# Three pieces of work in another order in a two-layer block on one core: a load ahead of two stores, a difference ahead of an eviction, half of a gram ahead of a mix

## The reference

```python
def layer0(v, gamma):                      # v = _gn(x)
    a = v.reshape(b, h * w, c)
    attn = softmax(einsum('bpi,bpj->bij', a, a))
    return gamma * einsum('bpc,bcj->bpj', a, attn) + a

def layer1(v, ...):                        # v = _gn(x + layer0)
    v = (v - v.min()) / (v.max() - v.min() + EPS)         # over each image
    measures = [box_sum(v, k) for k in (2, 4, 8, 16)]
    log_m = log(measures + EPS)
    alphas = einsum('bhwcs,s->bhwc', log_m, lr_c) / sum(lr_c ** 2)
    excite = sigmoid(relu(alphas.mean(h, w) @ w1 + b1) @ w2 + b2)
    sim = correlation of log_m with its fitted line
    return sim * sigmoid(bn(alphas)) + (1 - sim) * v * excite

x = x + layer0(_gn(x)); x = x + layer1(_gn(x))
```

## Time and profile before

| | |
|---|---|
| median of 3 timed runs | 6843.75 us (6843.52 to 6863.24) |
| the profiled execution | 6870.93 us, its span 6869.2 us |
| busy share of the span | VectorE 80%, TensorE 74%, ScalarE 70%, GpSimd 26% |
| DMA | 1344.69 MB moved, mean 196 GB/s |
| 695 us of turn 6 | VectorE busy 636.19, TensorE 581.42, ScalarE 579.68; granted clock 0.97 |

### The profile page before, as it was taken

How to read it: one execution, slowest core, us unless ns; L and a number is a source line. 1 busy time by engine, 2 the same in 40 slices (tenths; PEclk the granted TensorE clock), 3 DMA queues, 4 the chain that set the end, 5 groups by cost and what they waited for, 6 DMA issues and landing times. The chain is left out here.

```text
span 6869.2 us, 108733 instructions
## 1 busy us (share of the span) xinstructions
PE 5112.8 (74%) x35320; PEld 4647.5 (68%) x35320; DVE 5524.0 (80%) x6453; ACT 4827.6 (70%) x5203; POOL 1757.7 (26%) x1201
## 2 busy tenths in 40 slices
PE   6968886788858888588867888588885777466643
PEld 6757776677747777477766777477774666466642
DVE  1359998689969999699986999689996999699961
ACT  0118887588848888488875888488884888588861
POOL 0022221422232222322213222322223222333310
PEclk9989998899979999799988999799997999788875
DMA  3635554577746777477755777467774666456656
GB/s 117 195 114 166 176 171 130 176 232 240 230 148 214 226 232 230 132 235 230 223 190 169 238 241 228 148 208 228 236 230 126 219 221 220 159 170 187 189 176 230
DMA packets 874516, 1344.69 MB, mean 196 GB/s; under 512 B 38705, under 2 KB 694097, under 8 KB 857937
## 3 DMA queue, kind: packets, MB, share of 16 engines
q1 hardware_dynamic: 837456, 1208.16, 51.7%
q0 software_dynamic: 36864, 134.23, 10.3%
HBM read 671.16 MB, written 536.87 MB: 176 GB/s over the span
## 5 line engine op out<-in xcount | busy, mean ns | idle before, releaser
L530 PE MATMUL even<-band,t 128*128 128x128 f32 x12288 | 1867.0, 283 | 473.9 <-ACT logs L706 293.3
L530 PEld LDWEIGHTS even<-band,t 128*128 128x128 f32 x12288 | 1625.7, 197 | 548.6 <-issue 444.4
L387 POOL TENSOR_TENSOR t<-t 128x1024 f32<-128x1024 f32 (+3 forms) x800 | 1337.3, 1683 | 1451.3 <-DVE logs L979 1408.3
L511 PE MATMUL h_ps<-mix,xt 128*128 128x256 f32 x4096 | 1054.6, 403 | 454.0 <-DVE mx L891 327.3
L511 PEld LDWEIGHTS h_ps<-mix,xt 128*128 128x128 f32 x4096 | 773.8, 199 | 603.0 <-ACT xt L693 310.7
L428 POOL DMA_DIRECT2D x1t<-logs x256 | 226.4, 884 | 2882.9 <-DVE ut L990 2815.4
L706 ACT ACTIVATE logs<-even,col 128x1024 f32<-128x1024 f32 x512 | 568.8, 1111 | 444.6 <-PE even L530 443.2
L532 PE MATMUL even<-band,t 128*128 128x128 f32 x4096 | 792.0, 275 | 0.0
L891 DVE CUSTOM_DVE_ANT_0 h_out<-h_ps,shift,mx 128x512 f32<-128x512 f32 x512 | 382.7, 748 | 488.5 <-PE h_ps L511 487.5
L488 PE MATMUL g_ps<-xa 128*128 128x257 f32 x2048 | 634.8, 391 | 152.4 <-DMA xa<-in_x_dram 152.1
L532 PEld LDWEIGHTS even<-band,t 128*128 128x128 f32 x4096 | 621.9, 192 | 0.0
(11 more groups left out here) (184 smaller groups left out, 10492.4 us busy)
## 6 DMA issues: line engine op xcount, KB each, us to landing
xa<-in_x_dram SPq DMA_DIRECT2D x256, 512.0 KB, 4.5
xb<-in_x_dram SPq DMA_DIRECT2D x256, 512.0 KB, 5.5
h_scratch<-h_out SPq DMA_DIRECT2D x128, 1024.0 KB, 7.7
hr<-h_scratch SPq DMA_DIRECT2D x256, 512.0 KB, 6.0
q_scratch<-ut SPq DMA_DIRECT2D x256, 512.0 KB, 2.7
x1t<-logs POOLq DMA_DIRECT2D x256, 512.0 KB, 5.1
p_scratch<-x1t SPq DMA_DIRECT2D x256, 512.0 KB, 3.1
pd<-p_scratch SPq DMA_DIRECT2D x256, 512.0 KB, 6.1
```

The source lines that it names most:

```text
L387: ins = g.tensor_tensor(dst[:, hf, d:d + n, :], src[:, hf, d:d + n, :], src[:, hf, e:e + n, :], ALU.add)
L511: ins = t.matmul(h_ps[:, r * C:(r + 1) * C], xt[:, q % 2, jh, r, :], mix[:, jh, :], start=(jh == 0), stop=(jh == 1))
L530: ins = t.matmul(o, src[:, hf, at, :], band[:, which, :], start=True, stop=(which < 3))
```

## The change

Three edits, none of which adds or removes an instruction. On SyncE the load of h's rows, with its wait, goes ahead of the stores of h and out. On TensorE the second half of the gram goes from its place before box 3 to one between turn_back 0 and mix 2. On VectorE the third difference goes ahead of the second eviction of h_ps.

```diff
@@ SyncE, half_chunk
                     sp.dma_start(pd[:, hf, :], p_dram[ud]).then_inc(pq_loaded[hf], 16)
                     sp.dma_start(qd[:, hf, :], q_dram[ud]).then_inc(pq_loaded[hf], 16)
+                if Cs and not (began and hf == 0) and not (last and (k, hf) != (0, 0)):
+
+                    sp.wait_ge(odd_filled, 2 * u)
+                    apart()
+                    if hf == 1:
+                        load_rows(nC + 2, 1 - k, 0)
+                    else:
+                        load_rows(nC + 1, k, 1)
                 if Bs and hf == 0 and not began:
                     sp.wait_ge(h_copied, 4 * nb + 1)
                     apart()
...
                     sp.wait_ge(o_copied, 4 * nd + 1)
                     apart()
                     sp.dma_start(out_chunk[nd - 1], o_sb[:, 1 - k, :, :]).then_inc(o_stored[1 - k], 16)
-                if Cs and not (began and hf == 0) and not (last and (k, hf) != (0, 0)):
-
-                    sp.wait_ge(odd_filled, 2 * u)
-                    apart()
-                    if hf == 1:
-                        load_rows(nC + 2, 1 - k, 0)
-                    else:
-                        load_rows(nC + 1, k, 1)
                 if Cs and not began:
                     store_pq(u - 2, nC - 1, hf)
@@ TensorE, half_chunk
                     box(u, k, hf, 2)
                     box(u, k, hf, 1)
-                if A:
-                    gram_rows(n, hf, 1)
                 if Cs:
                     box(u, k, hf, 3)
...
                 if Ds:
                     turn_back(2 * nd + hf, hf, 0)
+                if A:
+                    gram_rows(n, hf, 1)
                 if Bs:
                     mix_x(nb, 2 * hf + 1)
@@ VectorE, half_chunk
                 if Cs:
                     low_contrasts(u, hf)
+                    high_contrast(u, hf)
                 if Bs:
                     copy_h(nb, k, 2 * hf + 1, first, None)
-                if Cs:
-                    high_contrast(u, hf)
                 if Bs:
                     min_h(i, k, hf)
```

## The result

The changed kernel takes 6643.64 us (four runs, 6641.73 to 6644.86), the one before 6843.64 us beside it (four runs, 6837.24 to 6863.24). The ratio is 0.9703, with a 95% interval of 0.9683 to 0.9723: 200 us faster. The forecast was 6637 us. Measured again beside the last experiments, against 6864.12 us for the kernel before, it took 6650.82 us, ratio 0.9697 (0.9678 to 0.9717).

What follows compares the result with a forecast made beforehand. VectorE was taken as the bound, so its waits could be won: 127 + 64 + 20 + 7 - 11 = 207 us off the timed median of 6843.75 us gives 6637 us, range 6598 to 6730 us, held at 78%.

Steps and rivals of the forecast that it cites:

- The bound: VectorE, busiest engine at 80% of the span, bounds the kernel with 21.1 us of work per half-chunk.
- The load of h's rows, 127 us: SyncE: issued ahead of both stores, the load lands in time and all L927 waits go, 127 us (low end 107).
- The reason of place: SyncE's queue: 2 MB of stores ahead made the load take 10.6 us against 5.9; moving it ahead gains 2.6 us.
- The waits for h_ps in full turns, 64 us: VectorE, turns 3 to 7: with the third difference first, copy_h's waits of 75 us shrink by 64 (low end 30).
- Turn 2, 20 us: VectorE, turn 2: of 41.8 us of waits for h_ps, mix 1's half stays; 20 us won, bounds 0 and 40.
- it starts only 0.15 us earlier, and TensorE idles there for the rest: TensorE: with the gram half moved away, box 3 still waits for log 2, so it gains only 0.15 us.
- The minimum behind the eviction, 11 us against: VectorE: min_h directly after the eviction it reads costs 0.05 us in 224 half-chunks, 11 us; bounds 0 and 25.
- Starts of turns, 7 us: TensorE, starts of turns 2 to 7: box 3 no longer behind the gram half; 7 us won, bounds 0 and 8.
- The load came earlier: Answers the rival that turn_h or the queue holds the load of h's rows: 127 us stay, 6764 us; 6%.
- the 6 us that I had named as a warning: Sign that the prediction is wrong: a summing DMA taking over 6 us.
- the 4.0 us of delay: Rival, stores stretch the summing DMA by 4.7 us, deciding from 4.0 us on: 62 us slower, 6906 us; 4%.
- The path behind xa: Rival: loop over summing DMA, SyncE, xa and mix 1, 20.5 us a half-chunk, takes over; 6757 us, 12%.

Runs made afterwards that it cites:

- the short minimum: Changed kernel with VectorE's minimum over h_out reading 16 elements per half-chunk instead of 1024 (values differ): 6484.07 us, ratio 0.9452 to the kernel before.
- The early xa: Changed kernel with the minimum cut to 16 elements and SyncE loading xa and xb ahead of the p and q stores: 6465.94 us, ratio 0.9427.

## Why the prediction was right, and where its terms were off

- **The bound.** VectorE at 21.1 us a half-chunk, with little beside it: turn 3 was to take 658 us and took 657.8. The clock of 1.00 over turn 3 is what I expected as well.
- **The load of h's rows, 127 us.** All waits went, and the part alone is worth 133 us. On top of the other two it is worth 110 to 115, since it and they share some 20 us. The load shown lands 7.8 us after issue where I allowed 8, 2.7 us early where I had 2.6. The reason of place was over-weighed: with one store ahead it would still have come in time. The earlier issue and the place of either store each did a part.
- **The waits for h_ps in full turns, 64 us.** They fell from 77.0 to 16.0 us, 61. With this term, the load's share in these turns (122 us) and 8 of the 11 us against, the five turns were to shorten by some 178 us; they did by 176.5. A wait of 2.2 us a turn was to stay, for mix 1 at the turn's start, and it did.
- **Turn 2, 20 us: this term was mis-sized.** I wrote "that half stays" of the waits for mix 1. They fell from 22.0 to 6.3 us, and the turn lost 35.1 us. The step that failed is that of the gram half leaving its old place: "it starts only 0.15 us earlier, and TensorE idles there for the rest", read from one half-chunk in which log 2 came late. The run without the gram's move shows the waits for mix 1 back (23.3 us). That half-chunk was not the rule even in its own turns: in each full turn of the trace before, box 3 started more than 0.5 us after log 2 had ended in 20 to 23 of 31 half-chunks.
- **The minimum behind the eviction, 11 us against: it came, a little larger.** The lists show no wait of L900, as they leave out idle times up to 0.15 us, but in the full turns it starts 0.12 us after the end of the instruction ahead of it, at the mean, where it had started 0.08 ahead of that end. The third difference wins 0.12 us of these 0.20 back in its new place. VectorE's time per half-chunk of the full turns, less its waits for h_ps and h's rows, is 21.13 us in the changed kernel and 21.06 without the difference's move: 0.07 us, some 15 in all.
- **Starts of turns, 7 us.** The stretches between the turns are 9 us shorter than before; without the gram's move all but 1 to 2 us of that is lost.
- **The rivals.** The load came earlier. The summing DMA takes 5.1 us at the median of the full turns and up to 6.6; 13 of 150 are over the 6 us that I had named as a warning, and before they were 12, up to 6.9. So the stores behind the load did not stretch it, and the 4.0 us of delay never came. The path behind xa is real, but in the changed kernel it cost at most some 2 us a full turn.

In sum the terms came to 207 us, measured are 200 (timed) and 229 (profiled). The 29 us between these two come almost wholly from the profiled execution of before, 27 us above the median of its runs. What made it so, no run here tells. That 207 lies so near to 200 is in part luck: the terms were read from the rows of that longer execution, in which turn 2 then gave 15 us more than its term, and they were taken off the shorter median.

## What to carry to other kernels

Take every short wait of the busiest engine, ask what queue or engine order put its releaser late, and check in the trace that the releaser could have gone earlier; then the sum of those waits is a good forecast, as long as no other path takes over. To see the next one, make the busiest engine lighter in a trial run and look which of its waits come back, and how often, not only at the mean. Ask of a moved piece what its old place frees, over all half-chunks of every stage and not in one. Look at the stretches between the loops too: what a loop wins can be lost there. Before work goes to GpSimd, look at which operands VectorE reads beside it.

## What the runs showed of the hardware that was not expected

A lighter VectorE can make a stretch slower. In turn 8, which has no gram, the kernel with the short minimum took 667.1 us for the 31 periods against 658.1 in the changed kernel, though VectorE had 1 us less to do in each. TensorE's waits there (line, released by: total us, times, longest):

```profile
PE even L530 <- ACT logs L706: 87.9, 31, 2.9
PE h_ps L511 <- ACT xt L693: 37.6, 31, 1.2
```

It idled 2.9 us for log 0 in every half-chunk, and the box that followed took 3.55 us where it takes 2.02 in the changed kernel:

```profile
5210.82 3.55 PE L530 MATMUL even<-band,t 128*128 128x128 f32 x16 [2.89 <-ACT logs L706]
```
```profile
5214.15 2.02 PE L530 MATMUL even<-band,t 128*128 128x128 f32 x16 [1.25 <-ACT logs L706]
```

The granted clock of turn 8 was 0.89 there, and 0.96 in the changed kernel:

```profile
4900.00:5500.00 600.00, 486.22 (x3329) 459.96 (x3329) 546.24 (x614) 515.86 (x556) 156.46 (x110) 0.89 0.67 216
```
```profile
5046.00:5700.00 654.00, 517.28 (x3684) 474.45 (x3682) 629.90 (x676) 571.38 (x616) 172.66 (x118) 0.96 0.66 213
```

So part of the time TensorE ran at the lower of its two levels, 1.2 GHz, after it had idled. It did not idle more in all: over the turn its waits come to 125.5 us there and 135.1 in the changed kernel. But there 30 of them are longer than 2.5 us, in the changed kernel 3. That this alone makes the 9 us is argued from the rows; no run here took the idle time away. The early xa on top changed little: 662.5 us, with 30 such waits again.
